# Attention context of two heads in half the array's columns each, with the softmax sums in a pass of their own

## The chip, the cores and the metric

The kernel runs on the 8 cores of one Trainium2 chip. Every core runs the same program on its own 1024 tokens (half of one of four sequences) and nothing is exchanged between cores. The metric is the device time of the slowest core in microseconds.

The engines of a core are named as the profile names them: PE is TensorE (PEld its weight loads), ACT is ScalarE, DVE is VectorE, POOL is GpSimd and SP is SyncE. PE multiplies a stationary operand, loaded by a weight load, with a moving operand that streams through it, and writes to PSUM.

## The reference

One transformer layer: pre-norm attention with 32 query heads and 8 key/value heads of 64 dimensions, then a feed-forward part with weights that are stored as integers. Cut to what matters here:

```python
q = (x @ Wq + bq)  # 32 heads of 64
k = (x @ Wk + bk)  # 8 heads, each used by 4 query heads
v = (x @ Wv + bv)
scores = jnp.einsum('bhqd,bhkd->bhqk', q, k) / np.sqrt(HEAD_DIM)
attn = jax.nn.softmax(scores, axis=-1)
ctx = jnp.einsum('bhqk,bhkd->bhqd', attn, v)
x = x + ctx @ Wo + bo
x = x + ((silu(g) * u) @ Wd)    # g, u = layernorm(x) @ Wg, Wu
```

## The kernel before

**Stages.** First x is normalised and transposed, and V and K are projected for all 2048 tokens of the sequence. Then comes the attention loop, which the change touches. After it stand the rest of the output projection with the second norm, and the long feed-forward part. Each engine has its own instruction list (`EL`), filled in the order in which the Python code runs, and engines meet only at semaphores.

**Attention loop.** The work is cut into 64 units of two heads and 256 queries: `units[u] = (qh, pj, qq)`. The two heads of a pair `pj` use two different key/value heads. A unit has 8 steps of 256 keys, so there are 512 steps `n`. Step `n` consists of

- `scores(n)`: four matmuls with 64 rows of the array each (a head has 64 dimensions). The two heads stand in different halves of the rows (`r = slice(64 * hh, 64 * hh + 64)`), and each matmul gives 128 keys x 256 queries. They fill two banks of PS_A, PS_B or PS_C, in turn.
- one exp on ACT over 128x1024 (`act_e[n]`), from PSUM into the bf16 tile `PT(n)`.
- `context(n)`: four matmuls over the full 128x128 array, one for each 128 keys and each head. `V128` holds for each head a block of 128 columns, 64 of V and 64 of ones, so that one matmul gives 64 rows of context and 64 rows that all hold the softmax sum. Head 0 lands in the columns 0 to 255 of `CT_BANK` (a bank of PS_D), head 1 in 256 to 511.

At the end of a unit DVE copies `CT_BANK` into `CTU(u)` and `divide(u, part)` does the rest on DVE in three parts, one for each later iteration: two reciprocals of 64x256 and then two multiplications of 64x256 into `CTXT`, the operand of the output projection.

**Order.** One iteration `k` of the loop puts on PE: the scores of steps 2k and 2k+1, the context of one, two or three older steps (`ctx_steps(k)`: 2k-3 and 2k-2, shifted so that a unit ends alone), and then some matmuls of a filler tile: a Q projection tile (`q_tile`) or an output projection tile (`w_tile`), 16 matmuls of 128x512 each, 44 tiles in all, dealt out by `share` and `count` over the iterations 4 to 255. With one context step an iteration gets about five filler matmuls, with two about three, with three about one. A filler tile waits until DVE has emptied the other bank of PS_D (`fill_free`). The rest of the order is fixed by the waits in `scores` (the exp of step n-3 must be done) and `context` (its own exp, and for a unit's first step DVE's copy of the bank).

```python
            for n in ctx_steps(k):
                context(n)
                if n % 8 == 7:
                    todo += [(n // 8, p) for p in range(3)]
```

Of the kernel before, what the change touches and what calls it, by code (L numbers as in the profile page):

```python
# [13 lines left out]
ALU = mybir.AluOpType  # L14
AX = mybir.AxisListType

P = 128
# [19 lines left out]
def _heads_of_pair(pj):  # L37
    j2, i = divmod(pj, 4)
    return 8 * j2 + i, 8 * j2 + 4 + i


def build_program():
# [22 lines left out]
    with ExitStack() as ctx:  # L65
# [10 lines left out]
        def bfv(off, cols):  # L76
            return vb[:, off // 2: off // 2 + cols]

        def f32v(off, cols):
            return vf[:, off // 4: off // 4 + cols]  # L80
# [35 lines left out]
        DVE = SEM["DVE"]  # L116
# [20 lines left out]
        def _wait(lst, sem, val):  # L137
            if val > 0:
                if isinstance(sem, str):
                    sem = SEM[sem]  # L140
                lst.append(lambda e, s=sem, v=val: e.wait_ge(s, v))

        def t_wait(sem, val):
            _wait(EL["t"], sem, val)

        def v_wait(sem, val):
            _wait(EL["v"], sem, val)
# [10 lines left out]
        def mm(out, l, r, start, stop, inc=False, skip=False):  # L158
            if inc:
                C['pe'] += 1  # L160
                EL["t"].append(lambda e, o=out, ll=l, rr=r, a=start, b=stop, k=skip:
                               e.matmul(o, ll, rr, start=a, stop=b,  # L162
                                        skip_group_check=k).then_inc(PE, 1))
            else:
                EL["t"].append(lambda e, o=out, ll=l, rr=r, a=start, b=stop, k=skip:
                               e.matmul(o, ll, rr, start=a, stop=b,  # L166
                                        skip_group_check=k))
            return C['pe']
# [25 lines left out]
        def v_op(name, *args, inc=False, chain=False):  # L194
            if chain:
                v_wait(DVE, C['dve'])
            if inc:
                C['dve'] += 1
                EL["v"].append(lambda e, n=name, a=args:
                               getattr(e, n)(*a).then_inc(DVE, 1))  # L200
            else:
                EL["v"].append(lambda e, n=name, a=args: getattr(e, n)(*a))  # L202
            return C['dve']
# [19 lines left out]
        def V128(t):  # L223
            return bfv((32 + 2 * t) * KB, 1024)

        def CTXT(qh, dc):
            return bfv((66 + 16 * qh + dc) * KB, 512)
# [17 lines left out]
        def PT(n):  # L245
            return bfv((146 + 2 * (n % 8)) * KB, 1024)
# [4 lines left out]
        def CTU(h):  # L251
            return f32v((170 + 2 * (h % 4)) * KB, 512)

        def REC(h):
            return f32v((178 + 2 * (h % 2)) * KB, 512)
# [6 lines left out]
        def half(ps, i):  # L262
            return ps[:, (i % 2) * 512:(i % 2) * 512 + 512]
# [224 lines left out]
        act_e, pe_s, pe_x, dve_ct, dve_nm = {}, {}, {}, {}, {}  # L488
        CT_BANK = half(PS_D, 0)
# [28 lines left out]
        def context(n):  # L518
            u, st = divmod(n, 8)
            j2 = units[u][1] // 4  # L520
            if n == 0:
                t_wait(GP, gp_ones)
            t_wait(ACT, act_e[n])
            if st == 0:
                t_wait(DVE, dve_ct[u - 1] if u else dve_q[3])
            for k2 in range(2):
                for hh in range(2):
                    c = hh * 512 + k2 * 256
                    mm(CT_BANK[:, hh * 256:(hh + 1) * 256],
                       V128(2 * st + k2)[:, (2 * j2 + hh) * P:  # L530
                                         (2 * j2 + hh + 1) * P],
                       PT(n)[:, c:c + 256],

                       start=(st == 0 and k2 == 0 and hh == 0),
                       stop=(st == 7 and k2 == 1),
                       inc=(k2 == 1 and hh == 1), skip=True)
            pe_x[n] = C['pe']
            if st == 7:
                v_wait(PE, pe_x[n])
                v_wait(DVE, dve_nm.get(u - 4, 0))  # L540
                dve_ct[u] = v_op("tensor_copy", CTU(u), CT_BANK, inc=True)

        dve_rc = {}

        def divide(u, part):
            qh, pj, qq = units[u]
            if part < 2:
                cs = slice(part * 256, part * 256 + 256)
                if part == 0:
                    v_wait(DVE, max(dve_ct[u], dve_nm.get(u - 2, 0)))  # L550
                dve_rc[u] = v_op("reciprocal", REC(u)[0:64, cs],
                                 CTU(u)[64:128, cs], inc=True)
                return
            v_wait(DVE, dve_rc[u])
            for hh, h in enumerate(_heads_of_pair(pj)):
                cs = slice(hh * 256, hh * 256 + 256)
                b = (h % 2) * 64
                dve_nm[u] = v_op(
                    "tensor_mul",
                    CTXT(qh, h // 2)[b:b + 64, qq * 256:qq * 256 + 256],  # L560
                    CTU(u)[0:64, cs], REC(u)[0:64, cs], inc=True)

        fill_free = {}
        fill_n = [0]
# [143 lines left out]
        def ctx_steps(k):  # L708


            n = [2 * k - 3, 2 * k - 2]
            if n[1] % 8 == 0:
                n = n[:1]
            if n[0] % 8 == 1:
                n = [n[0] - 1] + n
            return [m for m in n if 0 <= m < 512]
# [16 lines left out]
        for k in range(258):  # L733
            for n in (2 * k, 2 * k + 1):
                if n < 512:
                    scores(n)
            if k == 0:
                q_first(2)
                q_first(3)
            if k < 256 and k % 8 == 5 and k < 128:  # L740
                join_bo(k // 8)
            if k == 128:
                for w in range(4):
                    ld_xc(w)
            for n in ctx_steps(k):
                context(n)
                if n % 8 == 7:
                    todo += [(n // 8, p) for p in range(3)]
            if k in count:
                i_, c_ = count[k]  # L750
                if i_ not in run:
                    kind, t = FILL[i_]
                    if kind == "Q":
                        assert 2 * k + 2 >= 64 * (t // 4 - 2)
                    run[i_] = q_tile(t) if kind == "Q" else w_tile(t)
                for _ in range(c_):
                    next(run[i_])
            if todo:
                divide(*todo.pop(0))
        for t in todo:  # L760
            divide(*t)
# [520 lines left out]
        for c in range(32):  # L1282
# [8 lines left out]
            for tm in range(8):  # L1291
# [5 lines left out]
                for k in range(8):  # L1297
# [4 lines left out]
                       start=(cc == 0 and k == 0), stop=(cc == 7 and k == 7),  # L1302
                       inc=(k == 7))
                if cc == 7:
                    v_wait(PE, C['pe'])
                    if q == 0 and tm == 0:
                        v_wait("DSB", xd_dsb)
                    n = 8 * q + tm
# [6 lines left out]
                        inc=True, chain=True)  # L1315
# [119 lines left out]
```

## Time and profile before

| what | value |
|---|---|
| median of three runs | 2027.75 us (2027.48 to 2029.77) |
| the profiled execution's own time | 2026.54 us |
| its span on the slowest core (core 1) | 2025.0 us |
| PE busy | 1975.2 us, 98% |
| ACT busy | 1059.9 us, 52% |
| DVE busy | 1038.9 us, 51% |
| first to last exp of the attention loop | 164.9 to 733.7 us |

Busy times are sums over the whole span; the share in the attention loop is another one and is read from that stretch. A matmul's listed duration (some 0.27 us for 256 columns) includes its way through the array, so matmuls in a row overlap in the list. What one costs is the distance from its start to the start of the next.

### The profile page before, as it was taken

The numbers are of one execution on the slowest core, as the hardware profiler recorded it, in microseconds if no ns is written. First come the engines' busy times: TensorE is split into PE (matmuls) and PEld (weight loads), VectorE is DVE, ScalarE is ACT, GpSimd is POOL, SyncE is SP. The second block draws the span as 40 slices with busy tenths as digits, with TensorE's granted clock in tenths as the row PEclk, the third lists the DMA queues.
The fourth block names the chain that finished last, engine by engine and source line by source line (L and its number), as shares of the span: only waits on it lengthen the run. The fifth ranks groups of instructions, "written<-read, shape, count | busy, mean of one in ns | idle before, by whom it ended". The sixth has DMA issues, their size and how long they took to land.

```text
span 2025.0 us, 31971 instructions; the slowest of 8 cores (2020.3 to 2025.0 us)
## 1 busy us (share of the span) xinstructions
PE 1975.2 (98%) x11664; PEld 985.2 (49%) x11664; DVE 1038.9 (51%) x1425; ACT 1059.9 (52%) x1203; POOL 124.8 (6%) x177
## 2 busy tenths in 40 slices
PE   5999999999999999999999999999999999999999
PEld 3545555555555554444444444444444444444444
DVE  5624666666666667666666666666666102020202
ACT  2425889888888854544454444444544233223230
POOL 2000110110001100000000000000000000000000
PEclk9999999999999999999999999999999999999999
DMA  9628644442138348555555445544445857474651
GB/s 231 192 42 141 98 70 74 74 86 46 32 64 129 88 134 197 111 105 110 113 111 105 84 86 93 93 84 84 86 90 94 214 122 150 79 151 83 123 123 42
DMA packets 47382, 214.24 MB, mean 106 GB/s; under 512 B 5888, under 2 KB 5888, under 8 KB 30080
## 3 DMA queue, kind: packets, MB, share of 16 engines
q0 software_dynamic: 20160, 134.23, 38.8%
q1 hardware_dynamic: 27072, 77.98, 12.9%
q8 instruction: 99, 1.62, 0.3%
q14 instruction: 51, 0.42, 0.1%
HBM read 319.14 MB, written 27.26 MB: 171 GB/s over the span
## 4 chain that ended last, share of the span: by engine, by line
PE 93%; DMA 3%; DVE 2%; issue 1%; ACT 1%; DVEq 0%; ACTq 0%; POOLq 0%; SPq 0%
PE PS_B L166 22%; PE PS_D L166 20%; PE PS_C L166 20%; PE PS_A L166 19%; PE PS_D L162 4%; PE PS_B L162 3%; PE PS_C L162 2%; PE PS_A L162 2%; DMA arena<-wq 2%; DVE arena L200 1%; DMA arena<-wv 1%; PE PS_D L177 1%; DVE bns L200 1%; DVE arena L202 1%; DMA arena<-xt 0%
## 5 line engine op out<-in xcount | busy, mean ns | idle before, releaser
L166 PE MATMUL PS_D<-arena 128*128 128x256 bf16 (+1 forms) x2674 | 527.8, 320 | 14.3 <-DVE arena L200 11.2
L187 ACT ACTIVATE arena<-arena 128x1024 bf16<-128x1024 bf16 x384 | 379.9, 1048 | 289.2 <-DMA arena<-dwt 289.2
L166 PE MATMUL PS_B<-arena 128*128 128x512 bf16 (+1 forms) x2413 | 516.6, 357 | 0.2 <-DVE arena L200 0.2
L166 PE MATMUL PS_A<-arena 128*128 128x512 bf16 (+2 forms) x2175 | 458.8, 355 | 10.5 <-DMA arena<-wv 7.7
L166 PE MATMUL PS_C<-arena 128*128 128x512 bf16 (+1 forms) x2200 | 467.7, 354 | 0.8 <-ACT arena L187 0.8
L166 PEld LDWEIGHTS PS_B<-arena 128*128 128x128 bf16 (+1 forms) x2413 | 211.9, 97 | 259.7 <-issue 34.5
L187 ACT ACTIVATE arena<-PS_B 128x1024 bf16<-128x1024 f32 (+1 forms) x203 | 194.3, 957 | 265.8 <-PE PS_B L162 265.6
L166 PEld LDWEIGHTS PS_D<-arena 128*128 128x128 bf16 x2674 | 239.8, 98 | 177.0 <-issue 79.0
L200 DVE TENSOR_TENSOR arena<-arena 128x1024 bf16<-128x1024 bf16 (+2 forms) x500 | 301.8, 622 | 11.8 <-ACT arena L187 2.7
L200 DVE TENSOR_TENSOR arena<-PS_A,arena 128x512 f32<-128x512 f32 (+1 forms) x106 | 74.1, 699 | 455.0 <-PE PS_A L162 455.0
L166 PEld LDWEIGHTS PS_C<-arena 128*128 128x128 bf16 (+1 forms) x2200 | 190.8, 97 | 234.8 <-issue 34.3
L166 PEld LDWEIGHTS PS_A<-arena 128*128 128x128 bf16 (+1 forms) x2175 | 188.8, 98 | 238.6 <-issue 46.7
L200 DVE RECIPROCAL arena<-arena 64x256 f32<-64x256 f32 x128 | 215.7, 1721 | 5.6
L187 ACT ACTIVATE arena<-PS_C 128x1024 bf16<-128x1024 f32 (+1 forms) x202 | 193.1, 956 | 29.6 <-PE PS_C L162 25.1
L187 ACT ACTIVATE arena<-PS_A 128x1024 bf16<-128x1024 f32 x171 | 175.1, 1024 | 31.7 <-PE PS_A L162 31.6
L162 PE MATMUL PS_D<-arena 128*128 128x256 bf16 (+1 forms) x622 | 180.6, 292 | 0.0
L162 PE MATMUL PS_B<-arena 128*128 128x512 bf16 (+1 forms) x415 | 138.6, 334 | 0.0
L162 PE MATMUL PS_C<-arena 128*128 128x512 bf16 (+1 forms) x400 | 133.0, 332 | 0.0
L162 PE MATMUL PS_A<-arena 128*128 128x512 bf16 (+2 forms) x381 | 125.8, 330 | 0.0
L200 DVE COPY arena<-PS_D 128x512 f32<-128x512 f32 (+1 forms) x65 | 44.9, 690 | 127.5 <-PE PS_D L162 126.7
L187 ACT ACTIVATE arena<-arena,gs2b 128x512 bf16<-128x512 f32 x64 | 46.3, 724 | 62.3 <-DVE arena L200 62.3
L200 DVE TENSOR_TENSOR arena<-PS_C,arena 128x512 f32<-128x512 f32 (+1 forms) x44 | 31.5, 716 | 89.5 <-PE PS_C L162 89.5
(45 smaller groups left out, 893.7 us busy)
## 6 DMA issues: line engine op xcount, KB each, us to landing
arena<-gwt POOLq DMA_DIRECT2D x32, 1024.0 KB, 9.0
arena<-uwt POOLq DMA_DIRECT2D x32, 1024.0 KB, 9.0
arena<-dwt POOLq DMA_DIRECT2D x32, 1024.0 KB, 9.8
arena<-xt SPq DMA_DIRECT2D x16, 1024.0 KB, 13.3
arena<-wq POOLq DMA_DIRECT2D x32, 512.0 KB, 7.6
arena<-wo POOLq DMA_DIRECT2D x6, 2048.0 KB, 24.6
arena<-xt SPq DMA_DIRECT2D x32, 256.0 KB, 7.1
x2d<-arena SPq DMA_DIRECT2D x32, 256.0 KB, 6.5
```

Source lines behind the costliest of these rows:

```text
L162: e.matmul(o, ll, rr, start=a, stop=b, skip_group_check=k).then_inc(PE, 1))
L166: e.matmul(o, ll, rr, start=a, stop=b, skip_group_check=k))
L177: e.transpose(o, i, identb[:]))
L187: e.activation(o, i, f, bias=b, scale=s)
L200: getattr(e, n)(*a).then_inc(DVE, 1))
L202: EL["v"].append(lambda e, n=name, a=args: getattr(e, n)(*a))
```

## The change

The context matmuls take only the 64 columns of V as weights. Head 0 writes the partitions 0 to 63 of `CT_BANK` and head 1 the partitions 64 to 127, both in the columns 0 to 255. A second pass over the same steps, `sums(n)`, multiplies 32 columns of ones with the same `PT(n)`; its four matmuls (two heads, two blocks of 128 keys) write four different groups of 32 partitions, in the columns 256 to 511. An iteration first does the context of all its steps and then the sums of all its steps. DVE now adds the two halves of the sums, takes one reciprocal of 64x256, and multiplies in four pieces of 32x256, since a reciprocal has 32 rows for each head.

```diff
             for k2 in range(2):
                 for hh in range(2):
                     c = hh * 512 + k2 * 256
-                    mm(CT_BANK[:, hh * 256:(hh + 1) * 256],
+                    mm(CT_BANK[64 * hh:64 * hh + 64, 0:256],
                        V128(2 * st + k2)[:, (2 * j2 + hh) * P:
-                                         (2 * j2 + hh + 1) * P],
+                                         (2 * j2 + hh) * P + 64],
                        PT(n)[:, c:c + 256],
-                       start=(st == 0 and k2 == 0 and hh == 0),
-                       stop=(st == 7 and k2 == 1),
+                       start=(st == 0 and k2 == 0),
+                       stop=(st == 7 and k2 == 1), skip=True)
+
+        def sums(n):
+            u, st = divmod(n, 8)
+
+            for k2 in range(2):
+                for hh in range(2):
+                    c = hh * 512 + k2 * 256
+                    r = 64 * k2 + 32 * hh
+                    mm(CT_BANK[r:r + 32, 256:512], V128(2 * st + k2)[:, 64:96],
+                       PT(n)[:, c:c + 256], start=False, stop=(st == 7),
                        inc=(k2 == 1 and hh == 1), skip=True)
             pe_x[n] = C['pe']
...
         def divide(u, part):
             qh, pj, qq = units[u]
-            if part < 2:
-                cs = slice(part * 256, part * 256 + 256)
-                if part == 0:
-                    v_wait(DVE, max(dve_ct[u], dve_nm.get(u - 2, 0)))
-                dve_rc[u] = v_op("reciprocal", REC(u)[0:64, cs],
-                                 CTU(u)[64:128, cs], inc=True)
+            if part == 0:
+
+                v_wait(DVE, max(dve_ct[u], dve_nm.get(u - 2, 0)))
+                add = v_op("tensor_tensor", REC(u)[0:64, 0:256],
+                           CTU(u)[0:64, 256:512], CTU(u)[64:128, 256:512],
+                           ALU.add, inc=True)
+                v_wait(DVE, add)
+                dve_rc[u] = v_op("reciprocal", REC(u)[0:64, 256:512],
+                                 REC(u)[0:64, 0:256], inc=True)
                 return
-            v_wait(DVE, dve_rc[u])
-            for hh, h in enumerate(_heads_of_pair(pj)):
-                cs = slice(hh * 256, hh * 256 + 256)
-                b = (h % 2) * 64
+            hh = part - 1
+            h = _heads_of_pair(pj)[hh]
+            if hh == 0:
+                v_wait(DVE, dve_rc[u])
+            for r in (0, 32):
+                b = (h % 2) * 64 + r
                 dve_nm[u] = v_op(
                     "tensor_mul",
-                    CTXT(qh, h // 2)[b:b + 64, qq * 256:qq * 256 + 256],
-                    CTU(u)[0:64, cs], REC(u)[0:64, cs], inc=True)
+                    CTXT(qh, h // 2)[b:b + 32, qq * 256:qq * 256 + 256],
+                    CTU(u)[64 * hh + r:64 * hh + r + 32, 0:256],
+                    REC(u)[32 * hh:32 * hh + 32, 256:512], inc=True)
...
             for n in ctx_steps(k):
                 context(n)
+            for n in ctx_steps(k):
+                sums(n)
                 if n % 8 == 7:
                     todo += [(n // 8, p) for p in range(3)]
```

On PE an iteration with two context steps reads as follows before (L166 and L162 are the two lines of the helper `mm`, the second for a matmul that raises the semaphore; PS_A, PS_B and PS_C are scores, PS_D with 256 columns is context, PS_D with 512 columns the filler; a shape is that of the output):

```order
L166 MATMUL PS_D<-arena 128x256 x3
L162 MATMUL PS_D<-arena 128x256
L166 MATMUL PS_D<-arena 128x256 x3
L162 MATMUL PS_D<-arena 128x256
L166 MATMUL PS_D<-arena 128x512 x3
L166 MATMUL PS_A<-arena 128x256 x3
L162 MATMUL PS_A<-arena 128x256
L166 MATMUL PS_B<-arena 128x256 x3
L162 MATMUL PS_B<-arena 128x256
```

And the same piece of the program after the change, again two context steps and three filler matmuls:

```order
L166 MATMUL PS_D<-arena 64x256 x8
L166 MATMUL PS_D<-arena 32x256 x3
L162 MATMUL PS_D<-arena 32x256
L166 MATMUL PS_D<-arena 32x256 x3
L162 MATMUL PS_D<-arena 32x256
L166 MATMUL PS_D<-arena 128x512 x3
L166 MATMUL PS_A<-arena 128x256 x3
L162 MATMUL PS_A<-arena 128x256
L166 MATMUL PS_B<-arena 128x256 x3
L162 MATMUL PS_B<-arena 128x256
```

The eight context matmuls are narrower, eight matmuls of 32 columns of weights stand between them and the filler, and only the last of each step's sums raises the semaphore.

On DVE one unit of the first half of the loop reads as follows before, from its copy of the bank to the next unit's:

```order
L200 COPY arena<-PS_D 128x512 [waits PE,DVE]
L200 RECIPROCAL arena<-arena 64x256 [waits DVE]
L200 RECIPROCAL arena<-arena 64x256
L200 TENSOR_TENSOR arena<-arena 64x256 [waits DVE]
L200 TENSOR_TENSOR arena<-arena 64x256
```

And after:

```order
L200 COPY arena<-PS_D 128x512 [waits PE,DVE]
L200 TENSOR_TENSOR arena<-arena 64x256 [waits DVE]
L200 RECIPROCAL arena<-arena 64x256 [waits DVE]
L200 TENSOR_TENSOR arena<-arena 32x256 [waits DVE]
L200 TENSOR_TENSOR arena<-arena 32x256 x3
```

An add has come in, one of two reciprocals has gone, and the two multiplications have become four. ACT, SP and POOL have the same instructions in the same order.

## Rows read from the trace of the kernel before

**Rows 1.** The page: span, and busy time, share and instructions of each engine.

```profile
span 2025.0 us, 31971 instructions; the slowest of 8 cores (2020.3 to 2025.0 us)
PE 1975.2 (98%) x11664; PEld 985.2 (49%) x11664; DVE 1038.9 (51%) x1425; ACT 1059.9 (52%) x1203; POOL 124.8 (6%) x177
```

**Rows 2.** The chain that ended last: shares of the span by engine.

```profile
PE 93%; DMA 3%; DVE 2%; issue 1%; ACT 1%; DVEq 0%; ACTq 0%; POOLq 0%; SPq 0%
```

**Rows 3.** Busy time by stretch: attention loop, second norm, feed-forward.

```profile
core 1: us, PE busy (x) PEld busy (x) DVE busy (x) ACT busy (x) POOL busy (x), PEclk, DMA share, GB/s
164.40:733.70 569.30, 554.10 (x4809) 327.56 (x4809) 370.29 (x403) 494.35 (x510) 57.28 (x63) 0.99 0.45 81
733.70:860.00 126.30, 122.77 (x666) 59.95 (x663) 89.02 (x131) 54.45 (x74) 5.63 (x8) 0.99 0.70 169
860.00:2025.00 1165.00, 1160.73 (x5378) 526.03 (x5376) 502.65 (x776) 461.86 (x537) 46.45 (x88) 1.00 0.53 105
```

**Rows 4.** Timeline, PE, PEld and ACT, one iteration with three context steps.

```profile
399.65 0.81 PE L166 MATMUL PS_D<-arena 128*128 128x512 bf16 x3
...
402.35 0.39 PE L166 MATMUL PS_C<-arena 64*128 64x256 bf16 x3
...
402.47 0.20 PEld L166 LDWEIGHTS PS_A<-arena 64*128 64x128 bf16 x3
...
402.58 0.38 PE L166 MATMUL PS_A<-arena 64*128 64x256 bf16 x3
...
402.84 1.02 ACT L187 ACTIVATE arena<-PS_C 128x1024 bf16<-128x1024 f32 x1
...
402.89 0.50 PE L166 MATMUL PS_D<-arena 128*128 128x256 bf16 x3
...
403.34 0.49 PE L166 MATMUL PS_D<-arena 128*128 128x256 bf16 x3
...
403.76 1.02 ACT L187 ACTIVATE arena<-PS_A 128x1024 bf16<-128x1024 f32 x1
...
404.21 0.38 PE L166 MATMUL PS_D<-arena 128*128 128x512 bf16 x1
...
404.52 0.39 PE L166 MATMUL PS_B<-arena 64*128 64x256 bf16 x3
```

**Rows 5.** Waits of PEld in the attention loop: us in total, times, longest.

```profile
PEld PS_D L166 <- issue: 79.0, 297, 2.7
PEld PS_A L166 <- issue: 36.6, 87, 2.5
PEld PS_C L166 <- issue: 34.3, 86, 1.1
PEld PS_B L166 <- issue: 33.0, 84, 0.4
```

**Rows 6.** Costliest groups in the attention loop, by form: busy, mean ns.

```profile
L200 DVE RECIPROCAL arena<-arena 64x256 f32<-64x256 f32 x126 | 212.3, 1721 | 5.5
L200 DVE TENSOR_TENSOR arena<-arena 64x256 bf16<-64x256 f32 x124 | 50.3, 443 | 5.6
L200 DVE COPY arena<-PS_D 128x512 f32<-128x512 f32 x63 | 43.5, 690 | 127.0 <-PE PS_D L162 126.7
L166 PEld LDWEIGHTS PS_D<-arena 128*128 128x128 bf16 x2212 | 194.5, 98 | 123.8 <-issue 79.0
```

**Rows 7.** Waits of PE in the attention loop: us in total, times, longest.

```profile
PE PS_D L166 <- DVE arena L200: 11.2, 20, 1.2
```

**Rows 8.** Timeline, PE and DVE, where a filler tile waits for DVE.

```profile
382.18 0.74 DVE L202 TENSOR_SCALAR arena<-PS_D,bq2b 64x512 bf16<-64x512 f32 x1 [2.09 <-PE PS_D L162]
...
382.88 0.27 PE L162 MATMUL PS_D<-arena 128*128 128x256 bf16 x1
382.94 0.76 DVE L200 TENSOR_SCALAR arena<-PS_D,bq2b 64x512 bf16<-64x512 f32 x1
...
383.94 1.02 PE L166 MATMUL PS_D<-arena 128*128 128x512 bf16 x4 [0.79 <-DVE arena L200]
```

## The prediction

> **What bounds the kernel now.** I read the page first: PE is busy for 98% of the span [rows 1], and the chain that ended last is PE for 93% [rows 2]. A busy share of PE says little by itself, since overlapping matmuls count as busy. So I cut the span by stage [rows 3]. The attention loop, the only part that the change touches, lasts 569.3 us; behind it come 126.3 and 1165.0 us in which PE is busy for 97% and more, at a granted clock of 0.99 and 1.00 like the loop's 0.99. What the loop gains or loses is therefore handed to the end nearly one for one.
>
> Inside the loop two engines are candidates. ACT does 512 exps. Each lasts 1.02 us but two in a row start 0.92 us apart (402.84 and 403.76) [rows 4], so ACT needs at least 512 x 0.92 = 471 us. The loop's 569 us are 98 us more. An iteration (256 hold context) takes about 569 / 256 = 2.2 us, and ACT needs 1.84 us of it. DVE is busy 370 of 569 us [rows 3]. So PE sets the pace, and it would go on doing so until an iteration fell below 1.84 us.
>
> **What an iteration of PE is made of** [rows 4]. I take starts, never durations.
> - Eight context matmuls go from 403.34 to 404.21, so one costs 0.87 / 8 = 0.109 us.
> - A filler matmul costs 0.215 us: three of them span 0.81 us, one spans 0.38, and (0.81 - 0.38) / 2 = 0.215.
> - The four score matmuls of PS_C go from 402.35 to 402.58, 0.23 us, though each streams 256 columns like a context matmul. Four in a row would take 0.44. So two of them run at a time, one in each half of the rows: 0.11 us for a pair. This is the effect that the change wants in the columns.
> - From the start of PS_A's scores at 402.58 to the first context matmul at 402.89 pass 0.31 us where 0.22 are streaming. From the filler at 404.21 to the next scores at 404.52 pass 0.31 where 0.215 are streaming. So each **border between matmuls of 64 rows and matmuls of 128 rows costs 0.095 us**. Between context and filler, both 128x128, there is none.
> - The first matmuls behind a border take about 0.01 us more (0.50 against 0.49 for three context matmuls, 0.39 against 0.38 for scores), a weight load that nothing covers.
>
> That the borders are regular shows in the waits of PEld: 554 idle stretches that nothing in the profile releases [rows 5], against two borders in each of some 250 iterations.
>
> **The change part by part.**
> *Narrow context.* Per step four matmuls in a row become two pairs. If two column tiles run at a time as two row tiles do, a step goes from 4 x 0.109 to 2 x 0.109 us.
> *Sums.* Per step four matmuls of 32 columns, all four at a time if the same holds: one more 0.109 us. Together 512 x (4 - 3) x 0.109 = **-55.8 us**. The trace of before has no column tile, so the pace is bounded: best 0.109 for a pair and for four (the row pair), worst 0.109 for each matmul alone. I take the row pair, the nearest kind. For four, the later ones may start a little later; the bounds are nothing and 0.01 us, I take 0.005: 512 x 0.005 = +2.6 us.
> *New borders.* Context (128x64) to sums (128x32) comes up in 256 iterations, and sums to filler (128x128) in 252. The only borders that rows show change the number of rows; here only the columns change. Lower bound nothing, upper bound what a matmul's listed duration holds beyond its streaming, 0.27 - 0.109 = 0.16 us [rows 8]. I take the measured border, 0.095, as nearest: 508 x 0.095 = **+48.3 us**, with 0.01 for the uncovered load behind each: +5.1 us. The context's own border with the scores stays, but a narrow load stands behind it; I add another 0.01 in 256 iterations, +2.6 us, for which a full load of 0.098 us [rows 6] is the upper bound.
>
> The Trainium skill (TensorEngine Tiling (Array Packing), Key Properties) says that changing the tiling mode, and not just the tile, drains TensorE, and it lists 128x128, 128x64 and 128x32 as different modes. The trace agrees for row modes (0.095 us above); no run here shows it for columns yet. By that rule the sum is the one I make, without it -55.8 + 2.6 alone.
>
> *DVE.* A unit went from a copy (0.690), two reciprocals (1.721 each) and two multiplications (0.443 each), 5.02 us, to copy, add (priced as the multiplication of the same width), one reciprocal and four multiplications of the same 256 columns, 4.63 us [rows 6]. It is 25 us less over 64 units, but beside PE, which waits for DVE only 20 times for 11.2 us, at filler tiles [rows 7]. There the last context matmul starts at 382.88 and the filler only at 383.94, behind two bias additions of the previous tile, 0.74 and 0.76 us from 382.18 on [rows 8]. These begin when PE ends that tile, and no reciprocal is ahead of them, so a lighter DVE doesn't shorten this. In an iteration with one context step the change makes PE later by 2 x 0.095 - 0.109 + 0.02 = 0.10 us ahead of such a filler, which the wait swallows. I take half of the 20 waits: -1 us. The copy of the bank comes 0.1 us later, too; behind it stand about five filler matmuls (1.07 us) and the scores, cover for its 0.69.
>
> *PE's queue.* A step has twice the matmuls and weight loads. Four loads and four matmuls must fit 0.109 us; rows show two of each in it (three loads 0.20 us long in all, started while PS_C's last pair streams) [rows 4]. I take that more fit, and price the failure below.
>
> *Sum.* -55.8 + 2.6 + 48.3 + 5.1 + 2.6 - 1 = +1.8 us. The profiled execution took 2026.54 us (1.5 beyond its span), so the sum gives 2028.3; the median of the runs stands 1.2 above the profiled one, so on the runs' scale it is 2029.5, and I forecast **2029 us**, no change. By kind of iteration it is no zero: with three steps about 0.1 us less, with two nothing, with one 0.1 more.
>
> **Rivals.**
> 1. *Column widths have no border.* Then 53 us of streaming are gained. An iteration falls to 2.0 us, still over ACT's 1.84, but fillers come about 0.2 us earlier and wait that much longer at some 20 places (4 us). 2027.75 - 53 + 4 = 1979 us. For it: pieces of a column don't meet those of another, so nothing forces a drain; the loads of one tile needn't wait. Against: the only change of shape in the trace costs 0.095 us each time. Half of it, a border only on the way back to 128x128 or only between 64 and 32: 1979 + 24 = 2003 us.
> 2. *Column tiles overlap only in part* (the slower side). Unlike a row pair, which reads 64 + 64 partitions, each column tile reads all 128 partitions, and each needs a weight load of its own. If four sums go as two pairs: 512 x 0.109 = +56, 2084 us in place of the sum's 2028. If nothing overlaps, a step costs 8 x 0.109 in place of 3 x 0.109: +279, 2307 us. It decides early: a step has three groups, so 0.003 us more for each of the 1536 groups is already +4 us, a loss that can be told. For it: nothing in the trace shows such tiles. Against: PS_C's pairs overlap fully.
>
> The Trainium skill (TensorE: Matmul & The Clock Gate, Part 3) gives 2.38x for three column tiles of 512 columns, not 3x. By it, an estimate, a group would cost 3 x 0.109 / 2.38 = 0.137 us, 28 ns more, and the sum would be 1536 x 0.028 = +43 us, 2071 us; no row here shows that.
>
> 3. *The load behind a border is longer with narrow weights*: up to 0.04 us at 764 entries, +31 us at most, 2059 us. It is the upper side of the likeliest case, not a case of its own.
>
> **How the numbers follow.** Borders at about 0.095 and full overlap: 0.57, its own range 2020 (all uncovered loads and staggering nothing, -7.5) to 2045 (uncovered loads of 0.03: 764 x 0.02 = +15). No border 0.12, half 0.10, partial overlap 0.21, of which half below 2065. The range from 1998 to 2065 takes the likeliest, the half border and the small cases of partial overlap: 0.57 + 0.10 + 0.10 = 0.77. A measurement here tells about 0.2%, 4 us, from no change. Faster: 0.12 + 0.10 + a tenth of 0.57 = 0.28. Slower: 0.21 + a third of 0.57 = 0.39. Same: 0.33.
>
> **What would show it.** In the profile after, the loop should still last about 570 us. In the timeline, eight context matmuls of 64 columns should span four times 0.109, four sums start within 0.01 us, and gaps of 0.095 stand on both sides of the sums. If the starts of sums and fillers follow with no gap, the first rival holds; if the second of a pair starts 0.1 us behind the first, the second. DVE's busy time should fall by about 25 us with no effect. I would be wrong, above all, if a border in columns cost another amount than one in rows.

## The result

The changed kernel takes 2033.84 us (median of 14 runs), the kernel before 2030.72 us in the runs beside it; the ratio is 1.0029, with an interval from 1.0019 to 1.0039. It is slower by 0.3%, some 6 us. On both sides a few runs with a disturbed die are left out of the ratio.

The page of the profiled execution, the lines that answer to [rows 1] and [rows 2]:

```profile
span 2032.2 us, 36259 instructions; the slowest of 8 cores (2024.5 to 2032.2 us)
PE 1978.5 (97%) x13712; PEld 920.8 (45%) x13712; DVE 1032.4 (51%) x1553; ACT 1060.0 (52%) x1203; POOL 124.1 (6%) x177
PE 93%; DMA 3%; DVE 3%; issue 1%; ACT 0%; DVEq 0%; ACTq 0%; POOLq 0%; SPq 0%
```

2048 matmuls more, and PE is busy only 3.3 us longer than before. The stages, of core 5, the slowest here (as [rows 3]):

```profile
164.40:740.50 576.10, 556.09 (x6841) 263.82 (x6842) 364.90 (x530) 494.55 (x511) 58.21 (x65) 0.99 0.41 81
740.50:867.00 126.50, 122.40 (x680) 58.45 (x678) 88.08 (x132) 54.26 (x74) 5.27 (x8) 0.99 0.68 169
867.00:2032.20 1165.20, 1161.22 (x5381) 526.23 (x5378) 502.88 (x777) 461.89 (x537) 46.44 (x88) 1.00 0.52 105
```

The loop lasts 576.1 us in place of 569.3, the two stages behind it 126.5 and 1165.2 as before. All of the difference arises in the loop. The next view is the timeline of PE in one iteration with one context step and the following one with three (core 5; the second answers to [rows 4]):

```profile
405.92 0.39 PE L166 MATMUL PS_A<-arena 64*128 64x256 bf16 x3
...
406.46 0.63 PE L166 MATMUL PS_D<-arena 128*64 128x256 bf16 x7
406.81 0.28 PE L162 MATMUL PS_D<-arena 128*32 128x256 bf16 x1
407.02 1.04 PE L166 MATMUL PS_D<-arena 128*128 128x512 bf16 x4
...
407.99 0.39 PE L166 MATMUL PS_C<-arena 64*128 64x256 bf16 x3
...
408.53 1.07 PE L166 MATMUL PS_D<-arena 128*64 128x256 bf16 x15
...
409.32 0.28 PE L162 MATMUL PS_D<-arena 128*32 128x256 bf16 x1
...
409.43 0.28 PE L166 MATMUL PS_D<-arena 128*32 128x256 bf16 x3
409.44 0.27 PE L162 MATMUL PS_D<-arena 128*32 128x256 bf16 x1
...
409.54 0.28 PE L166 MATMUL PS_D<-arena 128*32 128x256 bf16 x3
409.55 0.27 PE L162 MATMUL PS_D<-arena 128*32 128x256 bf16 x1
409.75 0.39 PE L166 MATMUL PS_D<-arena 128*128 128x512 bf16 x1
...
410.07 0.39 PE L166 MATMUL PS_B<-arena 64*128 64x256 bf16 x3
```

- The four sums of a step start within 0.01 us (409.54 and 409.55), and the next four 0.11 us later (409.43 to 409.54). Four column tiles run at a time.
- From 408.53 to 409.32 stand twelve context matmuls and a border: 0.79 us. Six pairs at 0.109 are 0.65, which leaves 0.14 for the border, the load behind it that nothing covers and the starts inside the groups. Pairs run at a time as well.
- From the last four sums at 409.55 to the filler at 409.75 pass 0.20 us where 0.11 are streaming: a border of 0.09 to 0.10 us. In the first iteration it is 406.81 to 407.02, the same.
- The iteration takes 410.07 - 407.99 = 2.08 us; its like before took 2.17 (402.35 to 404.52 in [rows 4]). The one ahead of it, with one context step and four filler matmuls, takes 2.07 us from its first score at 405.92 to 407.99. Its like before took 1.95, from the row below (core 1) to 402.35 in [rows 4]. So an iteration with three steps gained 0.09 us and one with one step lost 0.12, where the prediction had 0.1 and 0.1.

```profile
400.40 0.39 PE L166 MATMUL PS_A<-arena 64*128 64x256 bf16 x3
```

So both halves of the prediction's sum are in the trace. The waits of PEld at which nothing releases it, as in [rows 5]:

```profile
PEld PS_D L166 <- issue: 167.5, 717, 4.7
PEld PS_A L166 <- issue: 35.0, 87, 2.5
PEld PS_C L166 <- issue: 32.8, 86, 1.1
PEld PS_B L166 <- issue: 31.9, 84, 0.8
```

420 stretches have come in at PS_D, the bank of context, sums and filler, and none at the scores. (The sum had 508 new borders.) And PE's own waits in the loop, as in [rows 7]:

```profile
PE PS_D L166 <- DVE arena L200: 11.4, 19, 0.9
PE PS_D L166 <- DMA arena<-wq: 4.5, 1, 4.5
PE PS_D L166 <- issue: 1.1, 5, 0.2
```

DVE is waited for as long as before (11.2 us). The wait for the Q weights' DMA, one wait in the whole loop, has something behind it that the sum did not have. Core 3, whose wait is 4.1 us, reads there (columns as in [rows 3]; the third number from the end is the granted clock):

```profile
204.00:206.00 2.00, 0.00 (x0) 0.00 (x0) 0.80 (x2) 0.68 (x1) 0.00 (x0) 1.00 1.04 140
208.00:210.00 2.00, 2.00 (x14) 0.63 (x12) 0.00 (x0) 0.53 (x1) 0.01 (x1) 0.50 0.99 151
210.00:212.00 2.00, 2.00 (x12) 0.54 (x8) 1.07 (x2) 1.41 (x2) 0.00 (x0) 0.50 0.99 203
```

PE stands still, and behind the stop its granted clock is 0.50, half speed (1.2 in place of 2.4 GHz), before it is back at 1.00. In the kernel before, with a wait of 3.4 us at the same place, the clock falls too but is at 0.88 again from 210 to 212. The time that a low clock costs is estimated here as time x (1 - granted clock), added up over rows of 2 us: 1.7 us in the loop before and 3.4 in the loop after, on core 3.

### The profile page after: what moved, and what is told of

It reads as the page before. It is cut to its first block, busy times and chain, and to the rows that moved or that the text cites. A ratio compares the mean times of both kernels' runs of the same rounds, so it can differ in the third digit from the quotient of the medians.

```text
span 2032.2 us, 36259 instructions; the slowest of 8 cores (2024.5 to 2032.2 us)
## 1 busy us (share of the span) xinstructions
PE 1978.5 (97%) x13712; PEld 920.8 (45%) x13712; DVE 1032.4 (51%) x1553; ACT 1060.0 (52%) x1203; POOL 124.1 (6%) x177
## 4 chain that ended last, share of the span: by engine, by line
PE 93%; DMA 3%; DVE 3%; issue 1%; ACT 0%; DVEq 0%; ACTq 0%; POOLq 0%; SPq 0%
PE PS_B L166 22%; PE PS_D L166 22%; PE PS_C L166 20%; PE PS_A L166 19%; PE PS_B L162 3%; PE PS_C L162 2%; PE PS_A L162 2%; DMA arena<-wq 2%; DVE arena L200 2%; PE PS_D L162 1%; DMA arena<-wv 1%; PE PS_D L177 1%; DVE arena L202 1%; DMA arena<-xt 0%; DVE bns L200 0%
## 5 line engine op out<-in xcount | busy, mean ns | idle before, releaser
L166 PE MATMUL PS_D<-arena 128*64 128x256 bf16 (+2 forms) x4722 | 533.3, 304 | 18.0 <-DVE arena L200 11.4
L166 PE MATMUL PS_B<-arena 128*128 128x512 bf16 (+1 forms) x2413 | 517.5, 357 | 0.3 <-DVE arena L200 0.3
L166 PE MATMUL PS_A<-arena 128*128 128x512 bf16 (+2 forms) x2175 | 460.4, 355 | 10.4 <-DMA arena<-wv 7.1
L166 PE MATMUL PS_C<-arena 128*128 128x512 bf16 (+1 forms) x2200 | 467.9, 355 | 0.8 <-ACT arena L187 0.8
L200 DVE TENSOR_TENSOR arena<-arena 128x1024 bf16<-128x1024 bf16 (+3 forms) x692 | 399.2, 583 | 25.2 <-ACT arena L187 3.5
L166 PEld LDWEIGHTS PS_D<-arena 128*64 128x64 bf16 (+2 forms) x4722 | 224.3, 102 | 256.4 <-issue 168.8
L166 PEld LDWEIGHTS PS_B<-arena 128*128 128x128 bf16 (+1 forms) x2413 | 212.0, 97 | 258.9 <-issue 33.8
L166 PEld LDWEIGHTS PS_A<-arena 128*128 128x128 bf16 (+1 forms) x2175 | 189.5, 98 | 238.1 <-issue 47.4
L166 PEld LDWEIGHTS PS_C<-arena 128*128 128x128 bf16 (+1 forms) x2200 | 190.8, 97 | 233.5 <-issue 32.8
L162 PE MATMUL PS_D<-arena 128*32 128x256 bf16 (+1 forms) x622 | 141.9, 296 | 0.0
L162 PE MATMUL PS_B<-arena 128*128 128x512 bf16 (+1 forms) x415 | 138.9, 335 | 0.0
L162 PE MATMUL PS_C<-arena 128*128 128x512 bf16 (+1 forms) x400 | 133.0, 333 | 0.0
L162 PE MATMUL PS_A<-arena 128*128 128x512 bf16 (+2 forms) x381 | 125.6, 330 | 0.0
L200 DVE RECIPROCAL arena<-arena 64x256 f32<-64x256 f32 x64 | 111.7, 1745 | 6.6
## 6 DMA issues: line engine op xcount, KB each, us to landing
arena<-xt SPq DMA_DIRECT2D x16, 1024.0 KB, 13.1
```

Source lines behind the costliest of these rows:

```text
L162: e.matmul(o, ll, rr, start=a, stop=b, skip_group_check=k).then_inc(PE, 1))
L166: e.matmul(o, ll, rr, start=a, stop=b, skip_group_check=k))
```

## The experiments

The table has, for core 3 of each profile, the loop's length (first to last start of an exp out of PS_A), what PE waited in it for DVE, for the Q weights' DMA and for nothing that the profile shows ("issue"), what the low clock cost (the estimate above), and under "rest" the loop less these four. The rest is where streaming and borders are. The ratio is that of the whole kernel's time to the kernel before, all cores and runs; the other columns are one core of one profile each. (Core 3 is a fair choice: on cores 0 and 6 of the changed kernel the trace has 127 matmuls fewer than weight loads, and 17 to 18 us of "issue" that are only missing records.)

| kernel | ratio (interval) | loop | DVE | DMA | issue | clock | rest |
|---|---|---|---|---|---|---|---|
| before | 1 | 568.0 | 11.2 | 3.4 | 0 | 1.7 | 551.7 |
| changed | 1.0029 (1.0019 to 1.0039) | 572.5 | 11.5 | 4.1 | 1.1 | 3.4 | 552.4 |
| all32 | 0.9992 (0.9981 to 1.0004) | 567.1 | 19.5 | 0 | 29.9 | 13.5 | 504.2 |
| fill32 | 0.9972 (0.9960 to 0.9985) | 561.6 | 13.5 | 4.4 | 7.1 | 3.4 | 533.2 |
| sums64 | 1.0140 (1.0122 to 1.0158) | 593.1 | 10.1 | 2.3 | 0.5 | 1.7 | 578.5 |
| before_fill64 | 1.0131 (1.0115 to 1.0147) | 593.3 | 10.9 | 1.5 | 0.2 | 1.7 | 579.0 |
| group2 | 0.9961 (0.9899 to 1.0024) | 559.4 | 17.1 | 2.4 | 0 | 1.7 | 538.2 |
| group2_bal | 0.9973 (0.9920 to 1.0025) | 560.7 | 19.6 | 0 | 0.2 | 1.5 | 539.4 |
| before_split | 1.0099 (1.0046 to 1.0152) | 590.6 | 11.2 | 0 | 10.5 | 5.1 | 563.8 |
| all32_noload | 0.9890 (0.9837 to 0.9942) | 545.4 | 20.5 | 0 | 15.6 | 6.9 | 502.4 |
| best_a | 0.9923 (0.9882 to 0.9965) | 550.5 | 18.8 | 3.4 | 7.1 | 1.7 | 519.5 |
| best_b | 0.9943 (0.9895 to 0.9991) | 550.8 | 19.7 | 2.5 | 6.1 | 3.4 | 519.1 |
| dve_more | 1.0143 (1.0076 to 1.0211) | 597.9 | 33.4 | 0 | 1.6 | 10.2 | 552.7 |

The edits below are shortened; `...` stands for lines left out.

**before_fill64**: one border more in the kernel before, nothing else.

```diff
-            mm(ps, WQ(k)[:, c * P:(c + 1) * P], HT(k // 16, c),
-               start=(c == 0), stop=(c == 15), inc=(c == 15))
+            if k < 4:
+                w = 128
+            for r in range(0, 128, w):
+                mm(ps[r:r + w, :], WQ(k)[:, c * P + r:c * P + r + w],
+                   HT(k // 16, c), start=(c == 0), stop=(c == 15),
+                   inc=(c == 15 and r + w == 128), skip=(w < 128))
```

(with `w = 64`, so that only the four tiles ahead of the loop stay whole, and the same in `w_tile`)

> The kernel before with only its filler tiles in two tiles of 64 columns side by side; context, sums and DVE are as before. This adds one border between column widths in each of 252 iterations and saves no streaming. Theory: 252 x 0.105 = 26 us and some 2 us of later starts, ratio to the kernel before 1.014 (2055 us). Rival (borders of column width alone cost nothing): within 3 us of the kernel before.

1.0131, and the rest of the loop grew from 551.7 to 579.0, 27.3 us for 252 borders: 0.108 us each, with the uncovered load and the later start of the second tile in it. A border between column widths costs what one between row heights does (0.095 and 0.01 for the load behind it [rows 4]), and the filler in column tiles costs no streaming. The rival is out.

**sums64**: the border between context and sums taken away, the sums streamed twice as long.

```diff
-                    r = 64 * k2 + 32 * hh
-                    mm(CT_BANK[r:r + 32, 256:512], V128(2 * st + k2)[:, 64:96],
+                    r = 64 * hh
+                    mm(CT_BANK[r:r + 64, 256:512], V128(2 * st + k2)[:, 64:128],
```

> The changed kernel with the sums in 64 columns of ones, two side by side, the same width as the context; the two heads' sums are then added to each other, so the division is by another number than the reference's. Theory: 256 borders of 0.1 us go, and the sums stream twice as long, 512 x 0.109 = 56 us more: 30 us above the changed kernel, ratio to the kernel before 1.018 (2064 us). Rival (a change of column width is free and the narrowest tiles are slow): close to the changed kernel, within 5 us.

1.0140, less than the 1.018 expected: the rest of the loop is 26.1 us over the changed kernel's, 30 were expected. Of the 56 us for the longer streaming 30 came back with the 256 borders between 64 and 32 columns, 0.12 us each. The rival is out.

**fill32** and **all32**: the added borders taken away one by one.

```diff
 # fill32: q_tile (here its q_mm, with w = 32) and w_tile
+            for r in range(0, 128, w):
+                mm(ps[r:r + w, :], WQ(k)[:, c * P + r:c * P + r + w],
...
 # all32: besides, context
+                    for r in (0, 32):
+                        mm(CT_BANK[64 * hh + r:64 * hh + r + 32, 0:256],
+                           V128(2 * st + k2)[:, (2 * j2 + hh) * P + r:
+                                             (2 * j2 + hh) * P + r + 32],
```

> The changed kernel with only the filler tiles in four tiles of 32 columns, so that the border from the sums to the filler is gone and the one from context to sums stays. Theory: 252 borders of 0.105 us come back, less some 5 us for starts in groups of four: 21 us below the changed kernel, about 0.992 of the kernel before (2012 us). Rival (only the border between 64 and 32 columns costs, or the narrow tiles do): same as the changed kernel or slower.

> The changed kernel with every 128-row matmul of the loop's iterations (context, sums, filler tiles) in tiles of 32 columns, four side by side, so that no border between column widths is left; the two borders with the scores stay. Theory (column borders of about 0.1 us each, 508 of them, ate the gain): about 53 us come back, less some 10 us for the later starts inside the groups of four; 40 us below the changed kernel, ratio to the kernel before 0.981 (about 1990 us). Rival (narrow tiles themselves cost more, through their weight loads or their reading of all partitions, not the borders): no gain, 2030 us or more.

The rest of the loop fell by 19.2 us in fill32 (21 expected) and by 48.2 in all32 (about 43 expected), 0.095 us for each of 508 borders: the borders were where the gain was. But the kernels gained only 0.57% and 0.37% over the changed one. In all32 PE stands 29.9 us without a releaser. One such place in the timeline of all32, with PE, PEld and ACT (core 3):

```profile
340.75 0.12 PEld L166 LDWEIGHTS PS_D<-arena 128*32 128x32 bf16 x8 [0.21 <-issue]
340.75 0.40 PE L166 MATMUL PS_D<-arena 128*32 128x256 bf16 x8
...
341.62 1.02 ACT L187 ACTIVATE arena<-PS_B 128x1024 bf16<-128x1024 f32 x1
343.56 0.23 PEld L166 LDWEIGHTS PS_D<-arena 128*32 128x32 bf16 x11 [2.70 <-issue]
343.57 0.51 PE L166 MATMUL PS_D<-arena 128*32 128x256 bf16 x11 [2.42 <-issue]
```

PE stops in the middle of a step's context matmuls, whose operands are there, for 2.4 us. The table by windows shows what DMA did around two of these stops (columns as in [rows 3], the last two DMA's busy share and GB/s):

```profile
340.00:342.00 2.00, 1.15 (x24) 0.43 (x16) 1.83 (x4) 2.00 (x3) 0.00 (x0) 1.00 0.82 281
342.00:344.00 2.00, 0.43 (x16) 0.43 (x20) 0.63 (x2) 0.64 (x1) 0.00 (x0) 1.00 0.06 18
...
444.80:447.40 2.60, 0.08 (x4) 0.00 (x1) 0.13 (x1) 0.70 (x1) 0.00 (x0) 1.00 1.01 366
```

In the second stop the DMA engines are at their fullest. In the first they are full as it begins, at 341.15, and nearly idle (0.06) for its last 1.5 us. So it is with the others: of the 14 stops of 0.7 us or more on this core, together 27 us, eight with 20 us lie where DMA's busy share is 0.85 or more (it is 0.41 over the loop), and four of 0.7 to 1.0 us where it is 0.00.

The long stops have a second price. The same eight filler matmuls take 0.61 us ahead of the second stop and 1.08 us behind it, where the granted clock is 0.60 (1.00 before):

```profile
444.28 0.61 PE L166 MATMUL PS_D<-arena 128*32 128x512 bf16 x8
447.40 0.39 PE L166 MATMUL PS_C<-arena 64*128 64x256 bf16 x3 [2.52 <-issue]
448.96 1.08 PE L166 MATMUL PS_D<-arena 128*32 128x512 bf16 x8
```

```profile
447.40:451.40 4.00, 4.00 (x60) 2.12 (x64) 0.00 (x0) 2.66 (x3) 0.00 (x0) 0.60 0.31 106
```

Over the loop of all32 the low clock costs 13.5 us, 10 more than in the changed kernel. With 28.8 us more of stops and 8.0 more of waits for DVE (and 4.1 less for the Q weights) this takes back 43 of the 48 us.

The view of the DMA queues has one that moves instructions: packets, MB, and share. In the loop of core 3 it is, before, changed and all32 in this order:

```profile
q8 instruction: 42, 0.69, 0.5%
```

```profile
q8 instruction: 57, 0.93, 0.7%
```

```profile
q8 instruction: 90, 1.47, 1.0%
```

So a third theory: PE uses up its instructions faster than they come, above all when their loads stand behind other DMA work. Two runs were made for it.

**before_split**: as many instructions as in fill32, with no tile and no border.

```diff
+                    for x in (0, 128):
+                        mm(CT_BANK[:, hh * 256 + x:hh * 256 + x + 128],
...
+                           PT(n)[:, c + x:c + x + 128],
 # and filler matmuls in four of 128 columns of the moving operand
```

> The kernel before with each context matmul cut into two of 128 columns of the moving operand and each filler matmul into four of 128, all still over the full array: no tile, no border, the same columns streamed, and as many instructions more on PE as in the run with fillers in four tiles (4160 matmuls and as many weight loads). Theory (PE runs out of instructions when it uses them up faster than they are loaded): idle stretches of 1 to 4 us on PE that nothing in the profile releases, together about 10 us; besides, each short matmul may cost 0.003 us or more, so 1.005 to 1.03 of the kernel before, and the stretches decide, not the time. Rival (such stretches come from column tiles): none longer than 1 us.

The stretches are there, in a kernel without a column tile. PE's waits of its core 1:

```profile
PE PS_D L166 <- issue: 11.1, 7, 2.7
PE PS_D L166 <- DVE arena L200: 10.7, 21, 0.9
PE PS_C L166 <- issue: 2.9, 1, 2.9
```

The number of instructions makes them, not the tiles. The longest, 2.9 us, ends at a score matmul at 231.84, and the DMA engines are nearly idle in it (0.08):

```profile
229.00:231.80 2.80, 0.00 (x0) 0.00 (x0) 0.00 (x0) 0.00 (x0) 0.00 (x0) 0.92 0.08 16
```

So full DMA engines can't be all of it. (The rest of the loop grew by 12.1 us, the price of 4160 short matmuls: 0.003 us each.)

**all32_noload**: fewer DMA transfers under the same instructions.

```diff
                     if k + 4 < 32:
-                        g_wait(PE, pe_q[k])
-                        ld_wq(k + 4)
+                        wd_wq[k + 4] = wd_wq[k]
```

> The kernel with all 128-row matmuls of the iterations in tiles of 32 columns, without the loads of the Q weights in the loop: the tiles from the ninth on use the four weight tiles that are there, so Q and all behind it are other numbers. Theory (instruction loads come late because the weight loads keep the DMA engines busy): the 22 to 34 us of idle stretches without a releaser on PE fall below 10 us, and the kernel gains 15 to 25 us, about 0.985 to 0.99 of the kernel before. Rival (PE can't take instructions at that rate, whatever DMA does): the stretches stay above 20 us and the time at 0.999.

The stretches fell from 29.9 to 15.6 us on core 3 and the ratio from 0.9992 to 0.989, though the instruction queue moves as much (91 packets against 90). Over the eight cores 22.5 to 33.7 us became 13.1 to 21.3. The theory asked for less than 10 us, so it falls short in size, but the rival's "whatever DMA does" is out. The low clock behind the stops cost 6.6 us less, and the rest is the same within 2 us (504.2 and 502.4): the gain is stops and clock, not borders. The other loads of the loop (x, output weights) are still there; that they hold up the remainder wasn't tried.

**group2** and **group2_bal**: half of the sums' passes.

```diff
             for n in ctx_steps(k):
                 context(n)
-            for n in ctx_steps(k):
-                sums(n)
...
+                pend.append(n)
+            if k % 2 == 1:
+                for n in pend:
+                    sums(n)
...
+                del pend[:]
```

> The changed kernel with the sums done only in every second iteration, for the context steps of two iterations: the same matmuls, and half of the added borders. Border theory: 254 borders and their uncovered loads fewer, 26 us below the changed kernel; some of it may go to iterations of uneven length, so 0.990 to 0.994 of the kernel before (2008 to 2016 us). Rival (what eats the gain is the number of narrow instructions): same as the changed kernel.

> As the run with sums in every second iteration, with the filler matmuls dealt out anew (about 4.5, 3, 3.4 and 1 in four iterations in a row) so that the iterations are equally long on PE. Border theory: 0 to 6 us below that run, about 0.990 of the kernel before. Rival (ACT evens out what PE does, or fillers wait more for DVE): no difference.

0.9961, with an interval that holds 1. The rest of the loop fell by 14.2 us, not 26. The expectation had a mistake of its own: in an iteration without sums there is still a border, from the context's 64 columns to the filler's 128. Only 127 borders went, some 13 us. The rival (the number of narrow instructions) fails in the rest, which fell with the same matmuls, but the ratios alone don't settle it. Dealing the fillers out evenly changed nothing that can be told (rest 539.4 against 538.2).

**dve_more**: a reciprocal twice per unit.

```diff
+                v_op("reciprocal", REC(u)[0:64, 256:512],
+                     REC(u)[0:64, 0:256], inc=True)
                 dve_rc[u] = v_op("reciprocal", REC(u)[0:64, 256:512],
-                                 REC(u)[0:64, 0:256], inc=True)
+                                 REC(u)[0:64, 0:256], inc=True, chain=True)
```

> The changed kernel with its reciprocal of each unit done twice, 64 x 1.72 = 110 us more on DVE. Theory (DVE's load is beside PE; only what stands in front of a filler tile's bias additions or the copy of the bank counts): 0 to 6 us slower than the changed kernel, 1.003 to 1.006 of the kernel before. Rival (DVE's work per unit paces the loop, so the lighter DVE of the change hid a loss): 15 us or more slower, 1.010 and up.

1.0143, 23 us over the changed kernel (10 to 37 by its interval): my theory (0 to 6 us) is wrong, and the time lies where the rival had it. PE's waits for DVE went from 11.5 to 33.4 us, though DVE was busy only 469 of 598 us of the loop. One of the five longest of these waits (core 3):

```profile
435.11 3.59 DVE L200 RECIPROCAL arena<-arena 64x256 f32<-64x256 f32 x2
438.73 0.74 DVE L202 TENSOR_SCALAR arena<-PS_D,bq2b 64x512 bf16<-64x512 f32 x1
439.49 0.76 DVE L200 TENSOR_SCALAR arena<-PS_D,bq2b 64x512 bf16<-64x512 f32 x1
440.50 0.81 PE L166 MATMUL PS_D<-arena 128*128 128x512 bf16 x3 [2.42 <-DVE arena L200]
```

```profile
442.00:444.00 2.00, 2.00 (x20) 0.87 (x19) 0.04 (x1) 1.68 (x2) 0.00 (x0) 0.50 0.74 225
```

Two reciprocals in a row hold the queue for 3.6 us, and the bias additions behind which a filler tile waits stand behind them. Behind this wait, too, the granted clock falls to 0.50, and it does so in all five places with a wait of 2.2 to 2.4 us; over the loop the low clock costs 6.8 us more than in the changed kernel. Waits and clock are the whole difference: the rest stays (552.7 against 552.4). DVE's order is on PE's path at the filler tiles; the rival's mechanism, that DVE's work as a whole paces the loop, isn't what the rows show, since 110 us more of it cost 23.

**best_a** and **best_b**: context and filler both at 64 columns, sums of two iterations together, straight behind the scores, where a border is anyway. 128 borders between column widths are left of 508.

```diff
+            pend += ctx_steps(k)
+            if k % 2 == 1:
+                for n in pend:
+                    sums(n)
+                del pend[:]
             for n in ctx_steps(k):
                 context(n)
-            for n in ctx_steps(k):
-                sums(n)
```

(with the filler of before_fill64; a unit's bank is copied behind its last context matmul, and `sums` waits for its exp itself)

> The changed kernel ordered so that few borders are left: filler tiles in two tiles of 64 columns like the context, and the sums (32 columns) of two iterations together in every second iteration, straight behind the scores, where a border is anyway. Borders between column widths: 128 in place of 508. Border theory: 380 x 0.1 = 38 us less streaming and gaps than the changed kernel; from what the earlier runs lost, 6 to 9 us go to filler tiles that then wait longer for DVE, and 2 to 4 us to late instructions, so 0.987 to 0.990 of the kernel before (2001 to 2008 us). Rival (each gain in the loop is swallowed by waits for DVE, DMA and instructions, as with all tiles at 32): 0.995 or more.

> The same with the filler matmuls dealt out as 4, 3, 3, 1 over four iterations, so that the iterations are equally long on PE. Border theory: the same gaps; a difference to the run with the old dealing within 4 us either way, by how many tiles then wait for DVE. Rival (uneven iterations make ACT idle and cost time): 5 us or more faster than with the old dealing.

best_a is faster than both kernels: 0.9923 (0.9882 to 0.9965), some 15 us below the kernel before. The rest of the loop fell by 32.9 us (38 expected). 7 us went to DVE, as foreseen, and 6 to stops without a releaser, more than the 2 to 4 foreseen. The ratio is above the expected 0.987 to 0.990; its interval still reaches that, and the rival's 0.995 as well. Its waits (core 3):

```profile
PE PS_D L166 <- DVE arena L200: 18.8, 29, 0.9
PE PS_D L166 <- issue: 5.3, 4, 2.4
```

The other dealing of fillers is no better (rest 519.1 against 519.5).

## Why the prediction was right, and where it was off

The forecast was 2029 us and no change; the kernel became 0.3% slower, just past what can be told from none. The direction of the sum (+1.8 us) was right, the chance for it (0.39; by its own terms 0.21 + 0.57 / 3 = 0.40) no more than the largest of three. That the sign came out is partly luck, as the last point shows.

- *Narrow context and sums, -55.8 us.* Right. Pairs and fours cost 0.11 us each in the timeline after, and before_fill64 streams its filler in pairs at no cost. The second rival (partial overlap) is out. The Trainium skill gives 2.38x for three column tiles of 512 columns (TensorE: Matmul & The Clock Gate, Part 3). No run here has such a pack, but nothing like it shows in fours of 256 columns: in a row they are 0.11 us apart, as one matmul would be.
- *New borders, +48.3 us.* Right, and the step on which all hung. In the trace after they cost 0.09 to 0.10 us, in before_fill64 0.108 with the load behind them. The Trainium skill (TensorEngine Tiling (Array Packing), Key Properties) says that a change of mode drains TensorE. The runs agree in that changes of column mode cost time as those of row mode do; that it is a drain, no row shows. The first rival is out.
- *The rest of the loop* in the table grew by 0.7 us. The terms without DVE add up to +2.8. So the streaming gained and the borders lost cancel even a little better than forecast.
- *DVE, -1 us.* Wrong in both halves. PE's wait for DVE didn't shrink (11.2 to 11.5 us). And DVE's busy time in the loop fell by some 6 us, not 25. I had priced by the mean duration of one, but of two reciprocals or multiplications in a row the second starts before the first ends: 212.3 / 126 = 1.685 and 50.3 / 124 = 0.406 us [rows 6]. After the change the same groups read

```profile
L200 DVE TENSOR_TENSOR arena<-arena 32x256 bf16<-32x256 f32 x250 | 111.1, 444 | 12.0
L200 DVE RECIPROCAL arena<-arena 64x256 f32<-64x256 f32 x63 | 109.9, 1745 | 6.5
L200 DVE TENSOR_TENSOR arena<-arena 64x256 f32<-64x256 f32 x63 | 35.0, 555 | 5.6
```

  and an add takes 0.555, not 0.443.
- *"A lighter DVE doesn't shorten this"* was argued from one place where no reciprocal was ahead. dve_more shows that this isn't general.
- *PE's queue, "I take that more fit".* Right within a step: 0.11 us held four loads and four matmuls. What more instructions cost came from elsewhere, as stops without a releaser: 1.1 us in the changed kernel, 29.9 in all32. No term of the sum had them. That they are late loads of instructions was argued, not shown.
- *What the measured 6 us hold.* Between the two profiles of core 3 the loop grew by 4.5 us: 0.7 in the rest, 1.7 by the low clock, 1.1 of stops, 0.7 a Q weight tile that came later, 0.3 DVE. Between the slowest cores of the two profiles (1 before, 5 after), read the same way, it grew by 5.6 us: 0.5 rest, 1.8 clock, 1.1 stops, 2.0 Q weights, 0.2 DVE. The sum had priced only the first and the last of these. In both pairs more than half of the growth is one longer wait for one weight tile and the half clock behind it; why that tile comes later after the change wasn't tried.

## What to carry to other kernels

Packing narrow matmuls side by side gives its full gain in streaming, but every change of tile shape costs about a matmul of 256 columns. Count the borders per iteration first, and give neighbouring work the same shape, even work that doesn't need it. Then look at what the freed time runs into: waits behind a queue on another engine, and stops that come with two or three times as many instructions. And read the granted clock behind every long stop of TensorE, since the stop can cost more than its length.

## What the runs showed of the hardware

- A change between column widths of 128, 64 and 32 costs TensorE 0.09 to 0.12 us, with the load behind it, and one between 64 and 128 rows about as much (0.095 and 0.01).
- Column tiles that read all 128 partitions each run fully at a time: four in 0.11 us for 256 columns.
- TensorE can stand still for up to 4.3 us with all operands there and no releaser in the profile: 0 us in the kernel before (core 3 throughout), 7.1 us with fillers in four tiles, 29.9 with everything in tiles of 32 columns, and 10.5 in a kernel without tiles and with as many instructions as the former. With the Q weights' loads gone, 29.9 became 15.6 us (all of these on core 3). That instruction loads come late behind other transfers fits the long stops with full DMA engines. It doesn't fit those with idle ones (2.9 us at a DMA share of 0.08 in before_split), whose cause stays open; the moment of each load against each stop isn't in the rows shown.
- Behind a stop of some 2 to 4 us TensorE's granted clock was often at 0.50 (1.2 GHz) for a few us: behind the Q weight wait of the changed kernel (4.1 us), in all five waits of 2.2 to 2.4 us of dve_more, behind the longest stops of all32. Not behind each: after the 2.4 us before 343.57 in all32 it stayed at 1.00. By the estimate above it cost 1.5 to 3.4 us of the loop in most kernels, 13.5 in all32 and 10.2 in dve_more.
